# A decoder layer's prologue: V's bias added on TensorE, V's parts read from PSUM, row transposes two groups ahead

## The reference

```python
x = x + attn(layernorm(x))          # Wq, bq, Wv, bv, anomaly_matrix A; 1 head
x = x + xattn(layernorm(x), ctx)    # 4 heads over 1601 context rows
x = x + ffn(layernorm(x))           # one of 4 experts per row

def attn(h):
    norm = ||h||;  s = h / (norm + 1e-9)
    q = s @ Wq.T + bq;  v = s @ Wv.T + bv
    scores = q @ (q @ A).T / 16
    return softmax(scores) @ v * norm
```

## Time and profile before

| | us |
|---|---|
| median of 3 runs (lowest, highest) | 826.67 (826.08, 827.56) |
| the profiled execution | 824.5 |
| its span | 822.3 |
| PE, DVE, ACT, POOL busy | 753.7, 629.5, 456.1, 165.8 |

### The profile page before, as it was taken

The page is one execution under the profiler, slowest core; times in us unless marked ns, Lnnn a source line. Parts: engine busy times, 40 slices in busy tenths (PEclk is TensorE's granted clock), DMA queues, the critical chain, the costliest instruction groups (busy, mean ns, idle before and its releaser), DMA issues. The chain is left out here.

```text
span 822.3 us, 19916 instructions
## 1 busy us (share of the span) xinstructions
PE 753.7 (92%) x6231; PEld 668.3 (81%) x6232; DVE 629.5 (77%) x1614; ACT 456.1 (55%) x924; POOL 165.8 (20%) x255
## 2 busy tenths in 40 slices
PE   4867978999999999999999999999997769999996
PEld 4766867888888888888888888888896658999996
DVE  5782835798888988889889898898886855777773
ACT  2444625766666666666666666666664712443342
POOL 3110022203123032130320312303122011222221
PEclk9888989999999999999999999999999969999999
DMA  6044074133131231321313303133167281111110
GB/s 218 5 139 142 0 271 141 57 110 108 40 128 67 77 106 38 132 89 49 106 40 130 106 32 111 58 108 106 38 225 305 98 326 28 36 41 39 41 32 16
DMA packets 51147, 80.95 MB, mean 98 GB/s; under 512 B 4894, under 2 KB 29216, under 8 KB 50976
## 3 DMA queue, kind: packets, MB, share of 16 engines
q1 hardware_dynamic: 49232, 75.63, 27.5%
q0 software_dynamic: 1872, 4.76, 1.6%
HBM read 45.60 MB, written 35.18 MB: 98 GB/s over the span
## 5 line engine op out<-in xcount | busy, mean ns | idle before, releaser
L1185 ACT ACTIVATE ps_cross<-flip 128x512 f16<-128x512 f32 (+1 forms) x256 | 124.8, 515 | 104.7 <-PE flip L897 83.5
L1409 DVE TENSOR_TENSOR ps_cross<-flip,ps_cross 128x512 f16<-128x512 f32 (+1 forms) x256 | 145.0, 584 | 29.9 <-ACT ps_cross L1185 29.0
L1370 ACT ACTIVATE exp_cross<-exp_cross,xneg 128x1024 f32<-128x1024 f32 (+1 forms) x128 | 122.7, 960 | 27.3 <-DVE xneg L1599 27.3
L897 PE MATMUL flip<-ident,exp_cross 128*128 128x128 f32 (+1 forms) x832 | 130.0, 279 | 6.7 <-DVE ps_cross L1409 3.6
L886 PE MATMUL scores<-keys_cross,qt 128*128 128x402 f32 x512 | 126.4, 369 | 3.6 <-ACT exp_self L1359 1.9
L897 PEld LDWEIGHTS flip<-ident,exp_cross 128*128 128x128 f32 (+1 forms) x832 | 94.0, 141 | 15.1 <-DVE ps_cross L1409 5.1
L739 PE MATMUL scores<-keys_self,u_tile 128*128 128x512 f32 x384 | 102.2, 403 | 4.1 <-issue 2.2
L908 PE MATMUL cross_out<-vals_cross,ps_cross 128*128 128x128 f16 (+1 forms) x832 | 100.7, 222 | 0.3 <-DVE ps_cross L1409 0.2
L910 PE MATMUL cross_out<-vals_cross,ps_cross 128*128 128x64 f16 (+1 forms) x832 | 94.0, 194 | 0.0
L873 PE MATMUL flip<-vals_self,ps_self 128*128 128x256 f16 x768 | 93.7, 276 | 0.0
L908 PEld LDWEIGHTS cross_out<-vals_cross,ps_cross 128*128 128x128 f16 (+1 forms) x832 | 75.4, 100 | 20.9 <-issue 14.7
(11 more groups left out here) (225 smaller groups left out, 1215.8 us busy)
## 6 DMA issues: line engine op xcount, KB each, us to landing
rows_dram<-pads SPq DMA_DIRECT2D x17, 520.0 KB, 4.0
w_piece<-W SPq DMA_DIRECT2D x32, 256.0 KB, 2.9
w_dram<-w_high SPq DMA_DIRECT2D x32, 256.0 KB, 2.3
w_dram<-w_piece SPq DMA_DIRECT2D x32, 256.0 KB, 2.7
w1s<-w_dram SPq DMA_DIRECT2D x8, 1024.0 KB, 12.6
w2s<-w_dram SPq DMA_DIRECT2D x8, 1024.0 KB, 12.5
u_dram<-u_out SPq DMA_DIRECT2D x4, 1024.0 KB, 5.9
u_tile<-u_dram SPq DMA_DIRECT2D x16, 256.0 KB, 2.7
```

Source lines behind the costliest of these rows:

```text
L897: tr = pe.transpose(flip[0:rows, bank(use), n * P:(n + 1) * P], exp_cross[:, h % 2, m * P:m * P + rows], ident[:, :])
L1185: return act.activation(out, in_, ACT.Copy, **kw)
L1370: act.activation(exp_cross[:, h % 2, cols], exp_cross[:, h % 2, cols], ACT.Exp, bias=xneg[:, h % 2, 1:2], scale=-1.0, accum_out=xden[:, ha ...
L1409: return dve.tensor_tensor(out, full, hi, ALU.subtract)
```

## The change

V's bias is accumulated in PSUM by two one-row matmuls per tile (a row of ones times the bias row's high and low part), so that `v_tmp` goes from the main path: ACT and DVE read V from PSUM, two tiles (one bank, 512 columns) per instruction. U of every group is written to scores 0 and 1. PE's order becomes U of g, transposes of g+2, V of g+1. DVE's order changes: statistics of group 1 and the bound come at other places, `scale_rows` and `statistics_pro` for later groups stand in front of `u_lo`, and the low parts of the cross-attention weights move one group later. PE meets the 8 bias columns, with their wait for the small loads, ahead of the first mixed product.

```diff
@@ gpsimd
-            if g == 2:
+            if g == 1:
                 pool.wait_ge(bound_step, 3)
                 pool.tensor_tensor(v_bound[:, 2:3], v_bound[:, 1:2], plus_half[:, 0:1], ALU.pow).then_inc(bound_rooted, 1)
@@ tensor
         tr.then_inc(wq_flipped, 1)
+        pe.wait_ge(bound_step, 2)
+        pe.matmul(scores[:, 3, 0:1], ones[:, :], bound16[:, :], start=True, stop=True).then_inc(bound_summed, 1)
         flip_x_pro(0)
+        pe.wait_ge(biases_loaded, 64)
+        for o in range(C):
+            for c in range(C):
+                mm = pe.matmul(cross_out[:, 8 + o:9 + o], w_raw[:, 2, c, o * P:(o + 1) * P], bq_col[:, c:c + 1],
+                               start=(c == 0), stop=(c == C - 1))
+        mm.then_inc(bias_mixed, 1)
         pe.wait_ge(self_w_lo, 2)
...
                 if g == 0:
                     pe.wait_ge(self_w_lo, 3)
+                    pe.wait_ge(bv_parts_set, 2)
+                    pe.wait_ge(bound_step, 3)
                 pe.wait_ge(pro_xt_lo, C * (g + 1))
                 if g and n % 2 == 0:
-                    pe.wait_ge(pro_v_biased, 4 * (g - 1) + n + 2)
...
+                    pe.wait_ge(pro_v_lo, 2 * (g - 1) + n // 2 + 1)
+                out = scores[:, 2 + n // 2, (n % 2) * D:(n % 2 + 1) * D]
+                for part in range(2):
+                    pe.matmul(out, one_row[:, :], bv_parts[:, part, :], start=(part == 0), stop=False)
+                three(out, lambda a, c: keys_self[:, a, c, (4 * g + n) * P:(4 * g + n + 1) * P],
+                      lambda b, c: w_self[:, 1, b, c, :], first=False).then_inc(pro_v_ready, 1)
...
-        self_u(0)
-        for g in range(1, GROUPS):
-            self_v(g)
+        for g in range(GROUPS):
+            self_u(g)
+            if g < GROUPS - 2:
+                flip_x_pro(g + 2)
             if g < GROUPS - 1:
-                flip_x_pro(g + 1)
-            self_u(g)
-
+                self_v(g + 1)
@@ scalar
+        def v_hi(g):
+            for n in range(2):
+                act.wait_ge(pro_v_ready, 4 * g + 2 * n + 2)
+                act.wait_ge(self_scale_step, 2)
+                act.activation(vals_self[:, 4 * g + 2 * n:4 * g + 2 * n + 2, 0, :],
+                               scores[:, 2 + n, :].rearrange("p (m d) -> p m d", m=2), ACT.Copy,
+                               scale=self_scale[:, 0:1]).then_inc(pro_v_hi, 1)
+
         xt_hi_pro(0)
+        act.wait_ge(biases_loaded, 64)
+        copy(bv_parts[:, 0, :], bv_row[0:1, :]).then_inc(bv_hi, 1)
         act.wait_ge(mixed_ready, 1)
         copy(mixed[:, 0, 0, :, :], scores[:, 1, :].rearrange("p (c n) -> p c n", c=C)).then_inc(mixed_hi, 1)
+        v_hi(0)
...
         for g in range(GROUPS):
+            if g:
+                v_hi(g)
             if g < GROUPS - 1:
                 xt_hi_pro(g + 1)
-            for n in range(4):
-                act.wait_ge(pro_v_biased, 4 * g + n + 1)
...
@@ vector
         statistics_pro(0)
-        statistics_pro(1)
+        dve.wait_ge(self_w_loaded, 48)
+        dve.tensor_tensor_reduce(v_tmp[:, :, :].rearrange("p c n -> p (c n)"), w_raw[:, 1, :, :].rearrange("p c n -> p (c n)"),
...
         scale_rows(0)
...
         low(w_self[:, 1, 1, :, :], w_raw[:, 1, :, :], w_self[:, 1, 0, :, :].bitcast(F32)).then_inc(self_w_lo, 1)
+        dve.wait_ge(bound_summed, 1)
+        dve.tensor_copy(v_bound[:, 1:2], scores[:, 3, 0:1]).then_inc(bound_step, 1)
+        dve.wait_ge(biases_loaded, 64)
+        dve.wait_ge(bv_hi, 1)
+        low(bv_parts[:, 1, :], bv_row[0:1, :], bv_parts[:, 0, :].bitcast(F32)).then_inc(bv_parts_set, 1)
+        statistics_pro(1)
+        dve.tensor_reduce(v_bound[:, 3:4], bv_row[:, :], AX.X, ALU.max, apply_absolute_value=True).then_inc(bound_step, 1)
         dve.wait_ge(mixed_hi, 1)
         low(mixed[:, 0, 1, :, :], scores[:, 1, :].rearrange("p (c n) -> p c n", c=C),
             mixed[:, 0, 0, :, :].bitcast(F32)).then_inc(mixed_lo, 1)
...
+        dve.tensor_copy(mixed_bias[:, 0, :], cross_out[:, 8:8 + C]).then_inc(mixed_bias_set, 1)
         scale_rows(1)
+        statistics_pro(2)
+        v_lo(0)
         dve.wait_ge(mixed_hi, 2)
         dve.scalar_tensor_tensor(out=mixed[:, 1, 1, :, :], in0=scores[:, 0, :].rearrange("p (c n) -> p c n", c=C), scalar=1.0 / 16.0,
                                  in1=mixed[:, 1, 0, :, :].bitcast(F32), op0=ALU.mult, op1=ALU.subtract).then_inc(mixed_lo, 1)
...
         for g in range(GROUPS):
+            if g:
+                v_lo(g)
             if g < GROUPS - 1:
                 xt_lo_pro(g + 1)
...
             if g == 0:
...
+                scale_rows(2)
+                statistics_pro(3)
+            if g == 1:
+                scale_rows(3)
             u_lo(g)

-            if g == 0:
+            if g == 1:
                 for dup in range(2):
...
-            if g == 1:
+            if g == 2:
                 for n, w in ((1, wv_cross), (2, wq_cross), (3, wo_cross)):
```

More of the change, by code:

```diff
@@ L163, in emit @@
     mixed_bias = sb("mixed_bias", [P, 2, C], F32, pro)
+    bv_parts = sb("bv_parts", [1, 2, D], F32R, pro)
+    one_row = sb("one_row", [1, P], F32R, pro)
     u_out = sb("u_out", [P, 4, 2 * C, P], F32R, pro)
@@ L267, in emit @@
     pro_v_ready = sem("pro_v_ready")
-    pro_v_biased = sem("pro_v_biased")
+    bv_hi = sem("bv_hi")
+    bv_parts_set = sem("bv_parts_set")
     pro_v_hi = sem("pro_v_hi")
@@ L751, in self_u @@
                     pe.wait_ge(u_lo_ready, C * (g - 1) + o + 1)
-                out = self_out if o == 0 else cross_out
-                three(out[:, :], lambda a, c: mixed[:, 1, a, c, o * P:(o + 1) * P],
+                three(scores[:, o, :], lambda a, c: mixed[:, 1, a, c, o * P:(o + 1) * P],
                       lambda b, c: keys_self[:, b, c, g * 512:(g + 1) * 512]).then_inc(pro_u_ready, 1)
@@ L798, in _ @@
         mm.then_inc(mixed_ready, 1)
[L799 to L806, removed]
         flip_x_pro(1)
         pe.wait_ge(mixed_bias_set, 1)
-        pe.wait_ge(bound_step, 3)
         for o in range(C):
@@ L1197, in u_hi @@
                     act.wait_ge(u_stored, 16 * g)
-                out = self_out if o == 0 else cross_out
                 act.wait_ge(mixed_bias_set, 2)
-                act.activation(u_out[:, :, o, :], out[:, :].rearrange("p (t s) -> p t s", t=4), ACT.Identity,
+                act.activation(u_out[:, :, o, :], scores[:, o, :].rearrange("p (t s) -> p t s", t=4), ACT.Identity,
                                bias=mixed_bias[:, 1, o:o + 1]).then_inc(u_hi_ready, 1)
@@ L1447, in u_lo @@
                 dve.wait_ge(u_hi_ready, C * g + o + 1)
-                out = self_out if o == 0 else cross_out
-                dve.scalar_tensor_tensor(out=u_out[:, :, C + o, :], in0=out[:, :].rearrange("p (t s) -> p t s", t=4),
+                dve.scalar_tensor_tensor(out=u_out[:, :, C + o, :], in0=scores[:, o, :].rearrange("p (t s) -> p t s", t=4),
                                          scalar=mixed_bias[:, 1, o:o + 1], in1=u_out[:, :, o, :].bitcast(F32), op0=ALU.add,
@@ L1453, in _, with v_lo @@
         dve.memset(ctx_t[:, :, :, M:MP].bitcast(F32), 0.0).then_inc(v_scale_step, 1)
-        statistics_pro(0)
-        statistics_pro(1)
+        dve.memset(one_row[:, :].bitcast(F32), 1.0).then_inc(bv_parts_set, 1)
+        def v_lo(g):
+            for n in range(2):
+                dve.wait_ge(pro_v_hi, 2 * g + n + 1)
+                dve.scalar_tensor_tensor(out=vals_self[:, 4 * g + 2 * n:4 * g + 2 * n + 2, 1, :],
+                                         in0=scores[:, 2 + n, :].rearrange("p (m d) -> p m d", m=2), scalar=self_scale[:, 0:1],
+                                         in1=vals_self[:, 4 * g + 2 * n:4 * g + 2 * n + 2, 0, :], op0=ALU.mult,
+                                         op1=ALU.subtract).then_inc(pro_v_lo, 1)
+        statistics_pro(0)
+        dve.wait_ge(self_w_loaded, 48)
+        dve.tensor_tensor_reduce(v_tmp[:, :, :].rearrange("p c n -> p (c n)"), w_raw[:, 1, :, :].rearrange("p c n -> p (c n)"),
+                                 w_raw[:, 1, :, :].rearrange("p c n -> p (c n)"), 1.0, 0.0, ALU.mult, ALU.add,
+                                 v_bound[:, 0:1]).then_inc(bound_step, 1)
+        dve.wait_ge(bound_step, 1)
+        dve.tensor_scalar(bound16[:, :], v_bound[:, 0:1], 1.02, None, ALU.mult).then_inc(bound_step, 1)
         scale_rows(0)
@@ L1483, in _ @@
-        dve.wait_ge(biases_loaded, 64)
         for g in range(GROUPS):
+            if g:
+                v_lo(g)
             if g < GROUPS - 1:
                 xt_lo_pro(g + 1)
-            if g < GROUPS - 2:
-                statistics_pro(g + 2)
             if g == 0:
[L1490 to L1516, removed]
```

39 lines of the change are left out of this document (17 added, 22 removed).

## The result

The changed kernel takes 830.87 us (median of 19 runs, 827.31 to 833.99) against 826.08 us (19 runs, 823.19 to 828.22) of the kernel before: ratio 1.0057, 95% interval 1.0045 to 1.0069. It is 4.8 us slower. I had forecast 826.8 and no change to speak of, with a range up to 829.0. The profiled execution took 832.69 us, with a span of 830.9.

A forecast was written before the change was run, and what follows sets the result against it. It took the first four slices to be bound by PE's front, then by rounds waiting for U's store; +3.1 - 2.0 - 0.6 - 0.4 = +0.1 us gave 826.8 us on the median, range 823.3 to 829.0.

The forecast's parts named there:

- the way from there to its store: From U of group 0 to its store: 2.0 us less without ACT's wait for V, 0.6 us less behind that.
- the rounds: Loop of store, U's parts and context part: two rounds of 10.84 and 11.31 us, together 0.4 us shorter.
- the front: PE's path from the first mixed product to U of group 0, forecast to end at 34.6 us, 3.1 us later.
- What bounds the kernel: From group 0's store on, each round waits for the store of U to land, as there is one u_out.
- The wait for the small loads: Ahead of PE's first product: wait to 14.66 us, then 8 bias columns in 2.0 us; product at 16.7 us.
- V of group 0: In PE's front: 24 + 8 matmuls in 4.8 us, from 19.6 to 24.4, one-row ones at full pace.
- with the same delay it rises at 20.8: In V of group 0: PE's clock rises about 4 us after the first product begins, as before.
- The fall in the thin stretch: Bias columns and transposes before U of group 0, 3.1 us: clock falls again, so U takes 5.5 us.
- I cost them at nothing: In the rounds: V before U, transposes two groups ahead and V's cheaper DVE parts only shorten work awaiting a store.
- the cover's limit: In the rounds: if the cover were gone, V and U matmuls would show, about 7 us a round against 9.5.
- Rival B: In PE's front: the wait for the small loads keeps the clock down through V of group 0; 829.8 us, chance 0.17.
- Rival A: Ahead of U of group 0: the clock does not fall, U takes 3.0 us; 824.3 us, chance 0.28.

The follow-up runs named there:

- e6: Changed kernel with V's bias put back on DVE through v_tmp, all new orders kept: 823.03 us, ratio 0.9973 to the kernel before.
- e7: Changed kernel with V's bias matmuls on 128 rows and the store of U ahead of the next context load: 812.75 us, ratio 0.9839 to the kernel before.
- e8: Kernel before with only the store of U moved ahead of the next context load on SP: 820.5 us, ratio 0.9937 to the kernel before.
- e1: Changed kernel without the eight one-row matmuls per group, V's bias left out of the output: 822.4 us, ratio 0.9966 to the kernel before.
- e2: Changed kernel with the same number of V bias matmuls, on 128 rows instead of one: 824.5 us, ratio 0.9985 to the kernel before.
- e12: Changed kernel, one-row matmuls kept, with the store of U ahead of the next context load: 825.4 us, ratio 0.9989 to the kernel before.
- e9: Changed kernel with V's bias matmuls on 64 rows instead of one: 826.04 us, ratio 1.0008 to the kernel before.
- e10: Changed kernel with 128-row bias matmuls in group 0 only, one-row ones in the other groups: 824.15 us, ratio 0.9992 to the kernel before.
- e11: Changed kernel with V's bias on DVE and the store of U ahead of the next context load: 817.6 us, ratio 0.9906 to the kernel before.
- e3: Changed kernel with the 8 bias columns back behind the second mixed product, one-row matmuls kept: 826.67 us, ratio 1.0039 to the kernel before.
- e5: Kernel before with V's bias by two one-row matmuls per tile, every order as before: 828.12 us, ratio 1.0046 to the kernel before.

## Why the prediction was wrong

The sum, term by term, at ACT's start of `v_f32` in the profiles: U of group 0 ends 4.7 us later (forecast 3.1), the way from there to its store is 2.6 us shorter (2.6), and the rounds are 2.8 us longer (forecast 0.4 shorter). That is 4.8 us for 0.1. Two terms failed: the front, and V in the rounds, which I had put at nothing. The second missed by more, 3.2 us against 1.6, since in the front two errors hid each other in part.

- **What bounds the kernel** was right in the main: the rounds follow the store. e6 shows them at the forecast length, e7 and e8 by taking the bound away. The landing of the store at 47.73 and 73.08 is in the changed kernel too. For group 1 of the kernel before I had read it too simply: ACT was idle for 0.25 us only before it started at 45.77, as V's high parts had held it till then, and e8 starts there no earlier.
- **The wait for the small loads** came as forecast: PE to 14.55, the 8 columns at twice their time, the first product at 16.28 (16.7).
- **V of group 0 failed**: 4.8 us forecast, 9.1 measured. It failed twice. The price of a one-row matmul was set at a full one's pace, 0.133 us, with 0.244 as upper end. A pair adds 0.59 us to a tile at the high clock (1.33 against the 0.74 of a plain one in e1), 0.30 a matmul. At the low one it adds 0.99 us (2.30 against the 1.31 of a plain one in V of group 2 before), 0.50 a matmul. Both are outside my bounds. The Trainium skill (TensorE: Matmul & The Clock Gate, LDWEIGHTS) has the load independent of the rows. The trace agrees: two loads take 0.50 us with one row and 0.54 with 128, at the low pace. But the load of the tall pair starts 0.2 us ahead of its matmul (19.29 for 19.50 in e2), and that of the one-row pair at its matmul (19.11 for 19.12), behind 0.22 us of idle time:

```profile
19.11 0.50 PEld L800 LDWEIGHTS scores<-bv_parts,one_row 1*128 1x128 f32 x2 [0.22 <-issue]
...
19.29 0.54 PEld L800 LDWEIGHTS scores<-bv_parts,one_row 128*128 128x128 f32 x2
```

- The other failure in V of group 0 is "with the same delay it rises at 20.8": by the pace the clock did not rise before V was over. This is the larger part. At the high pace V takes 5.3 us, one-row matmuls and all (e12), so 3.8 of the 9.1 us are the clock.
- **The fall in the thin stretch** did not come: U of group 0 took 3.0 us for 5.5. This hid 2.5 us of V's cost, and so U ended at 36.2, where I had 34.6. I had given the fall the better chance. It came in e1 (U 4.6 us), but not in e2, e6, e7, e9, e10, e11 and e12, which have the same stretch; what decides it stays open.
- **"I cost them at nothing"** for V in the rounds failed in one of three. I had named the cover's limit, 7 us of PE work a round against 9.5, at the high clock. At the low one transposes, V and U of group 2 took 15.1 us (47.3 to 62.4), and 2.8 us came out at the end.
- **Rival B** named the place (V of group 0 at the low clock to its end) and had 829.8 us for it, at 0.17. That it came within 1.1 us of the time is luck in part: it kept the slow U of group 0, which did not come, and had nothing for the round of group 2. Its cause is at most half the story: without one-row matmuls the same wait costs nothing that shows (e1), and with them V of group 0 can still run at the high pace (e9, e12). No chance stood on the clock being held down again in a later round.
- **Rival A** was right that the clock need not fall: e2 and e6 have U of group 0 in 3.0 us and are at 824.5 and 823.0 us, where A had 824.3. That the order itself is good shows in e6.

## What to carry to other kernels

A matmul's cost isn't its columns alone: here one of 1 or 64 rows among tall ones left the weight load idle around it, and a V with such matmuls stayed at the low clock once it was there. Pad a bias row to full height (ones divided by 128) before it goes among full matmuls. That alone brought the change back to the kernel before's time, not under it. And look at what waits for a DMA's completion before tuning the engines: moving one store ahead of one load was worth more than the whole reordering.

## What the runs showed of the hardware

- Two matmuls of 256 columns cost 0.43 us from start to start of the next at the high clock with 1 or 64 rows, 0.23 with 128; at the low one 0.72 and 0.43. The six full matmuls behind a short pair take longer too, at the high clock 0.90 us to the next start for 0.71.
- By the pace, the clock rose in V of group 0 about 5 us after the first product began with 128-row pairs (e2, 16.8 to 21.9). With one-row pairs it took 14 us in the changed kernel's profile, and rose only behind them; but in e12 it rose within 3 us, at the first pair.
- By the granted clock, low stretches with a V of 1-row or 64-row pairs in them lasted 10.2 us (e3, e9) and 13.7 us (changed kernel, e12), and ended behind V in all four. The low stretches without such a V lasted 6.8 us at most, in all profiles. With plain or tall matmuls in V of group 2 they ended inside V (e1, e2, e6, e7) or within 0.7 us behind it (kernel before, e8). Why the short matmuls do this was not tested: their empty rows and the idle time around them always came together.
- A V that begins at the high clock need not stay there: in e3 (one-row) and e2 (tall) it fell in the first tile of V of group 2, behind 2.1 and 2.3 us in which PE had waited for DVE. In e10 it did not fall behind the same wait.
- The single runs of e3, e5 and e9 fall into two groups with 2.3 to 3.4 us of nothing between them, so one kernel may meet either case from run to run. What decides it was not found.
